# A fused attention and mixture-of-experts kernel: second expert projection with the tokens as stationary side, three weight buffers, and reordered batch boundaries

## The reference

```python
inp = _ln_c(x) + 2.0 * sinu
q, k, v = conv2d(inp, wq), conv2d(inp, wk, 1, 1), conv2d(inp, wv, 1, 1)   # 1x1, 3x3, 3x3; 8 heads of 32
q = q * cos + rotate_every_two(q) * sin                                   # k likewise
attn = softmax(einsum('bhid,bhjd->bhij', q, k) * SCALE)                   # 1024 x 1024 a head
attn = einsum('bhij,hg->bgij', attn, mix)
out = einsum('bhij,bhjd->bhid', attn, v)
a, g = split(conv2d(out, wo) + bo, 2)
x = x + a * sigmoid(g)
# experts: E = 8, hidden 512, the two best of each token
h = gelu(einsum('end,edh->enh', layernorm(t) * ln_g + ln_b, W1) + b1)     # 128 -> 512
y = einsum('enh,ehd->end', h, W2) + b2                                    # 512 -> 128
t = t + (weights * the two chosen y).sum()
```

## Time and profile before

| | us |
|---|---|
| median of three executions | 2919.08 (2915.07 to 2923.99) |
| the profiled execution, its time | 2920.96 |
| its span, first instruction to last | 2919.2 |
| PE busy | 2782.3 (95%) |
| DVE busy | 2268.1 (78%) |
| ACT busy | 1465.8 (50%) |
| POOL busy | 1385.4 (47%) |

### The profile page before, as it was taken

One profiled execution on the slowest core, in us unless ns is written; L12 is line 12 of the kernel. 1 busy time (PEld: TensorE's weight loads), 2 busy tenths in 40 slices (PEclk: granted clock), 3 DMA queues, 4 the chain that ended last, 5 costly groups with the idle time before them and its releaser, 6 DMA issues.

```text
span 2919.2 us, 51230 instructions
## 1 busy us (share of the span) xinstructions
PE 2782.3 (95%) x20202; PEld 2602.2 (89%) x20202; DVE 2268.1 (78%) x3471; ACT 1465.8 (50%) x1883; POOL 1385.4 (47%) x1049
## 2 busy tenths in 40 slices
PE   6999999999999999999999999999999999997896
PEld 5899989998999899988999899989998999976676
DVE  6777788778878888878887787888778888764563
ACT  3455445553555355544555355535554455564561
POOL 4344433544445524653354344553465336456783
PEclk9999999999999999999999999999999999998998
DMA  2555030102111120202111211112010201156665
GB/s 110 202 197 215 8 98 23 33 24 94 37 38 58 62 67 25 73 23 84 37 40 45 95 37 39 57 63 54 24 44 30 76 23 54 53 176 216 208 213 205
DMA packets 98632, 237.89 MB, mean 81 GB/s; under 512 B 19960, under 2 KB 24642, under 8 KB 98406
## 3 DMA queue, kind: packets, MB, share of 16 engines
q1 hardware_dynamic: 89318, 217.85, 23.2%
q0 software_dynamic: 9088, 16.94, 1.7%
HBM read 131.23 MB, written 105.30 MB: 81 GB/s over the span
## 4 chain that ended last, share of the span: by engine, by line
PE 74%; DVE 9%; DMA 5%; issue 4%; POOL 3%; ACT 3%; SPq 1%; another core or an unknown queue 1%; POOLq 0%; DVEq 0%; ACTq 0%
PE PV L752 48%; PE ST L752 13%; PE MX L752 12%; DMA wt<-wall 2%; POOL acc L638 1%; DVE rt L1573 1%; DMA stk<-rt 1%; DMA qst<-stk 1%; ACT xr L1215 1%; DVE El L1608 1%; DVE tmp L1587 1%; ACT h L1215 1%; PE PV L860 1%; DMA y<-yrows 1%
## 5 line engine op out<-in xcount | busy, mean ns | idle before, releaser
L638 POOL TENSOR_TENSOR acc<-acc,tmp 128x256 f32<-128x256 f32 x512 | 801.3, 1565 | 1204.3 <-DVE tmp L1618 1202.3
L752 PE MATMUL PV<-vh,El 128*128 128x258 f32 x4096 | 1186.3, 290 | 9.8 <-DVE El L1608 4.5
L752 PE MATMUL PV<-vh,Eh 128*128 128x258 f32 x4096 | 1158.0, 283 | 0.0
L752 PE MATMUL PV<-vl,Eh 128*128 128x256 f32 x4096 | 1148.8, 280 | 0.0
L1215 ACT ACTIVATE Eh<-ST 128x1024 fp32r<-128x1024 f32 x512 | 524.6, 1025 | 735.1 <-PE ST L752 735.1
L1603 DVE TENSOR_REDUCE mcol<-MX 128x1 fp32r<-128x1024 f32 x512 | 625.5, 1222 | 254.4 <-PE MX L752 253.6
L752 PEld LDWEIGHTS PV<-vh,El 128*128 128x128 f32 x4096 | 772.8, 189 | 42.7 <-issue 10.9
L752 PEld LDWEIGHTS PV<-vl,Eh 128*128 128x128 f32 x4096 | 779.9, 190 | 24.6 <-issue 3.3
L752 PEld LDWEIGHTS PV<-vh,Eh 128*128 128x128 f32 x4096 | 774.5, 189 | 0.0
L1608 DVE TENSOR_TENSOR El<-E,Eh 128x1024 fp32r<-128x1024 f32 x512 | 641.4, 1253 | 0.4
L1215 ACT ACTIVATE E<-ST 128x1024 f32<-128x1024 f32 x512 | 521.6, 1019 | 0.0
(11 more groups left out here) (264 smaller groups left out, 3357.0 us busy)
## 6 DMA issues: line engine op xcount, KB each, us to landing
rows<-xr SPq DMA_DIRECT2D x68, 520.0 KB, 6.3
stk<-rt SPq DMA_DIRECT2D x64, 512.0 KB, 2.8
kst<-stk SPq DMA_DIRECT2D x192, 128.0 KB
qst<-stk SPq DMA_DIRECT2D x192, 128.0 KB
wt<-wall SPq DMA_DIRECT2D x39, 514.0 KB
wt<-wall SPq DMA_DIRECT2D x39, 512.5 KB
xrow<-rows SPq DMA_DIRECT2D x39, 260.0 KB
y<-yrows SPq DMA_DIRECT2D x32, 256.0 KB, 4.6
```

The source lines that it names most:

```text
L638: nc.gpsimd.tensor_tensor(acc[:, ic, :], acc[:, ic, :], tmp[:, p, :], ALU.add).then_inc(s_acc, 1)
L752: return nc.tensor.matmul(o, w, m, start=start, stop=stop)
```

## The change

`project` takes the hidden layer's parts as stationary side, 128 tokens at a time, and the weights as moving side of 128 columns, so that its results are token rows in PSUM; they go to two banks in turn. `y_out` and `y_transpose` are gone. DVE's `weight_out` adds the bias, which now stands in every row of the second weights (`WROW`), and then multiplies. Both weights have three buffers, and a load waits for the last reader of its own buffer. `load_mid` goes in halves and in tiles 21 to 36. `values` takes high x high, high x low and then low x high. The order of the calls in `batch` is another on PE, ACT and DVE, and the first batch's pairs are written out. The core of the diff (left out: semaphores and buffers renamed to match, the written-out pairs on the other engines, counts):

```diff
-WROW = (2 * HID + HK, 2 * HID + 1)
+WROW = (2 * HID + HK, 2 * HID + C)
...
+WB = 3
...
-        wt = [[keep(f"wt{i}{par}", [P, WROW[i]], f32r) for par in range(2)] for i in range(2)]
+        wt = [[keep(f"wt{i}{par}", [P, WROW[i]], f32r) for par in range(WB)] for i in range(2)]
...
-        yev = [keep(f"yev{i}", [P, NB], f32) for i in range(2)]
+        ysum = [keep(f"ysum{i}", [P, NB], f32) for i in range(2)]
...
+                sp.dma_start(wall_d[1][:, :, 2 * HID:2 * HID + C],
+                             b2.rearrange("e (o d) -> e o d", o=1).to_broadcast([EXP, P, C])).then_inc(t_wst, 16)
...
+            def load_mid(i):
+                half = slice(i % 2 * NB, (i % 2 + 1) * NB)
+                sp.dma_start(mid_sb[:, i // 2, half], mid_d[i // 2, :, half]).then_inc(t_mid, 16)
...
+            for j in range(WB):
+                load_w(0, j)
+            for j in range(WB - 1):
+                load_w(1, j)
...
-                if j + 2 < NT:
+                if j + WB < NT:
                     wait(sp, t_gl, 4 * j + 4)
-                    load_w(0, j + 2)
+                    load_w(0, j + WB)
...
-                if j + 2 < NT:
-                    wait(sp, t_ye, j + 1)
-                    load_w(1, j + 2)
+                if j + WB - 1 < NT:
+                    wait(sp, t_yw, j)
+                    load_w(1, j + WB - 1)
...
-                if 8 <= j < 8 + B:
-                    load_mid(j - 8)
+                if j >= NFULL and j < NFULL + 2 * B:
+                    load_mid(j - NFULL)
...
-            def values(n, k, p, jcs):
+            def values(n, k, p, jcs, low=None):
 
                 e = k % 2
+                hi, lo = ([t[:, e, jc, p * P:(p + 1) * P] for jc in range(KC)] for t in (Eh, El))
                 for jc in jcs:
                     if jc == 0:
                         wait(pe, s_nrm, 2 * n + p + 1)
                     if p == 0 and jc % 4 == 0:
+                        wait(pe, s_ex, 2 * n + jc // 4 + 1)
+                    mm(PV[p][:, 0:VW], hi[jc], vh[:, jc, :], jc == 0, False)
+                if low is not None:
+                    pe.wait_ge(s_vlo, low)
+                for jc in jcs:
+                    mm(PV[p][:, 0:INNER], hi[jc], vl[:, jc, :], False, False)
+                for jc in jcs:
+                    if p == 0 and jc % 4 == 0:
                         wait(pe, s_lo, 2 * n + jc // 4 + 1)
-                    hi, lo = (t[:, e, jc, p * P:(p + 1) * P] for t in (Eh, El))
-                    mm(PV[p][:, 0:VW], lo, vh[:, jc, :], jc == 0, False)
-                    mm(PV[p][:, 0:INNER], hi, vl[:, jc, :], False, False)
-                    last = mm(PV[p][:, 0:VW], hi, vh[:, jc, :], False, jc == KC - 1)
+                    last = mm(PV[p][:, 0:VW], lo[jc], vh[:, jc, :], False, jc == KC - 1)
...
                 conv_q(b, 1)
+                conv_q(b, 2)
+                conv_q(b, 3)
                 if prev is not None:
                     out_transpose(prev, 0)
-                conv_q(b, 2)
-                conv_q(b, 3)
                 conv(b, 0, 0)
+                conv(b, 0, 1)
                 if prev is not None:
                     out_transpose(prev, 1)
-                conv(b, 0, 1)
-                if prev is not None:
                     out_project(prev, 0)
                 conv(b, 0, 2)
                 conv(b, 0, 3)
                 conv(b, 1, 0)
                 conv(b, 1, 1)
                 conv(b, 1, 2)
+                conv(b, 1, 3)
                 if prev is not None:
                     out_project(prev, 1)
-                conv(b, 1, 3)
                 conv(b, 2, 0)
+                conv(b, 2, 1)
+                conv(b, 2, 2)
                 if prev is not None:
                     route_in(prev)
-                conv(b, 2, 1)
-                conv(b, 2, 2)
                 conv(b, 2, 3)
                 if prev is not None:
                     pe.wait_ge(s_xr, b + 0)
...
                 conv(b, 3, 2)
+                max_scores(n + 1, 1, 0)
                 scores(n, 0, 0, b)
-                max_scores(n + 1, 1, 0)
                 conv(b, 3, 3)
+                max_scores(n + 1, 1, 1)
                 scores(n, 0, 1, b)
-                max_scores(n + 1, 1, 1)
...
-                if prev is None:
-                    with pe.Fori(0, HEADS // 2 - 1) as hp:
-                        pair(n + hp * 8, heads_next(hp), split=b * 4 + 4)
-                else:
-                    for hp in range(HEADS // 2 - 1):
-                        pair(n + hp * 8, heads_next(hp), split=b * 4 + 4, route=prev if hp == 1 else None,
-                             through=b - WPREP if hp == 2 and 0 <= b - WPREP < EXP // 2 else None)
+                for hp in range(HEADS // 2 - 1):
+                    pair(n + hp * 8, heads_next(hp), split=b * 4 + 4, route=prev if hp == 1 else None,
+                         through=b - WPREP if hp == 2 and 0 <= b - WPREP < EXP // 2 else None)
...
-            def y_transpose(j):
-                wait(pe, t_ye, j + 1)
-                wait(pe, t_yw, j)
+            def project(j):
+
+                w = wt[1][j % WB]
+                wait(pe, t_w[1][j % WB], 16 * (j // WB + 1))
+                wait(pe, t_yw, j - 1)
+                wait(pe, t_hl, 2 * j + 2)
                 for i in range(4):
-                    last = nc.tensor.transpose(YT[:, i * P:(i + 1) * P], yev[j % 2][:, i * P:(i + 1) * P], ident[:, :])
-                last.then_inc(t_yt, 1)
-
-            def project(j):
-                w = wt[1][j % 2]
-                wait(pe, t_w[1][j % 2], 16 * (j // 2 + 1))
-                wait(pe, t_ye, j)
-                for k in range(HK):
-                    if k % 2 == 0:
-                        wait(pe, t_hl, 2 * j + k // 2 + 1)
-                    last = split3(Y, w[:, k * P:(k + 1) * P], w[:, HID + k * P:HID + (k + 1) * P],
-                                  hh[:, j % 2, k, :], hl[:, j % 2, k, :], k == 0, k == HK - 1)
+                    at = slice(i * P, (i + 1) * P)
+                    for k in range(HK):
+                        last = split3(PV[j % 2][:, at], hh[:, j % 2, k, at], hl[:, j % 2, k, at],
+                                      w[:, k * P:(k + 1) * P], w[:, HID + k * P:HID + (k + 1) * P], k == 0, k == HK - 1)
                 last.then_inc(t_y, 1)
...
-                if j > 0:
-                    y_transpose(j - 1)
                 project(j)
...
                 rot_hi(b, 1)
                 if prev is not None:
                     gate_tanh(prev, 0)
+                middle_copy(b, 0)
...
                 rot_hi(b, 4)
+                rot_hi(b, 5)
                 if prev is not None:
                     gate_tanh(prev, 1)
-                rot_hi(b, 5)
...
                 rotate(b, 0)
+                rotate(b, 1)
                 if prev is not None:
                     out_lo(prev, 0)
-                rotate(b, 1)
+                rot_lo(b, 0)
+                rotate(b, 2)
                 if prev is not None:
                     clear(prev)
-                rot_lo(b, 0)
-                rotate(b, 2)
                 rot_lo(b, 1)
                 rotate(b, 3)
                 middle_sums(b, 0)
                 even_odd(b, 0, 0)
-                rot_lo(b, 2)
                 if prev is not None:
                     gate(prev, 0)
+                rot_lo(b, 2)
+                even_odd(b, 0, 1)
+                if prev is not None:
+                    out_lo(prev, 1)
                 turn(b, 4)
                 rot_lo(b, 3)
-                if prev is not None:
-                    out_lo(prev, 1)
-                even_odd(b, 0, 1)
                 turn(b, 5)
                 middle_sums(b, 1)
-                if prev is not None:
-                    gate(prev, 1)
                 rot_lo(b, 4)
                 even_odd(b, 1, 0)
                 even_odd(b, 1, 1)
                 rot_lo(b, 5)
                 turn(b, 6)
+                if prev is not None:
+                    gate(prev, 1)
                 turn(b, 7)
                 middle_sums(b, 2)
+                rot_lo(b, 6)
                 even_odd(b, 2, 0)
                 if prev is not None:
                     logits(prev)
-                rot_lo(b, 6)
                 v_lo(b, 0)
+                take_max(n, 0, 0)
+                rot_lo(b, 7)
                 even_odd(b, 2, 1)
-                take_max(n, 0, 0)
+                take_max(n, 0, 1)
                 v_lo(b, 1)
-                rot_lo(b, 7)
-                take_max(n, 0, 1)
...
             def weight_out(j):
-                wait(dve, t_yt, j + 1)
+                wait(dve, t_y, j + 1)
                 if j >= YR:
                     wait(dve, t_sc[j % YR], 64 * (j // YR))
+                y, bias = ysum[j % 2].rearrange("p (i d) -> p i d", d=C), f(wt[1][j % WB][:, 2 * HID:2 * HID + C])
+                tt(y, PV[j % 2].rearrange("p (i d) -> p i d", d=C), rows(bias, 4, C), ALU.add).then_inc(t_ys, 1)
+                wait(dve, t_ys, j + 1)
```

(54 more changed lines are left out.)

36 lines of the change are left out of this document (11 added, 25 removed).

## The result

The changed kernel takes 2937.76 us in the median of seven runs (2933.86 to 2943.49), the kernel before 2919.08 on the same chip: a ratio of 1.007, 95% interval 1.005 to 1.009. It is slower by 0.7%, where the forecast was no measurable change, at 2917 us.

What follows compares the result with a forecast made beforehand. TensorE was taken as the bound, waiting mainly at batch boundaries and for weights in the expert stage. Expert stage with tail +25.5, boundaries -27.7, the rest 0: -2.2 us, about 2917 us; range 2900 to 2942.

Steps and rivals of the forecast that it cites:

- The projection: Expert tiles: 48 narrow pairs at 0.111 us plus change-over, 5.43 us a projection, making a tile 8.7 us of PE.
- The weights: Expert stage: with a third buffer the 18.1 us of waits for weights go; the middle stretch gains some 15.
- DVE sets the start of the pairs: Rival, boundaries: PE only waits elsewhere, so they give just -10 against +32 in the expert stage; about 2941 us, chance 0.20.
- The third buffer doesn't help: Rival, middle expert tiles: transfer rate, not late issue, binds them; the middle stays near 114 us, time 2934, chance 0.08.
- the granted clock falls to 1.2 GHz in the projections: Rival, expert projections: narrow pairs take about twice 0.111 us, +5.3 us a tile, 3120 us if always; chance 0.03.
- The boundaries: Seven boundaries between batches: reordered calls and a recovered clock, less time given back, sum -27.7 us, bounds -10 and -38.
- The stack's term: Boundaries: `gate(prev, 1)` goes behind `turn(b, 6)` on DVE, so the first stack's spill is issued sooner: -10.9 us.
- the clock's 10.3 us: Boundaries: 10.3 us lost to the granted clock falling behind waits; two thirds counted as regained, -7 us.
- the low part's term: Boundaries: `values` takes the low part last and needs `vl` and `El` later, saving about half their waits: -3.7 us.
- The accumulator's: Boundaries: `conv_q` 2 and 3, six wide matmuls of 1.4 us, go under the 1.84 us accumulator wait: -9.8 us.
- The rest: First batch's loop passes written out and the bias table written once: taken as 0, between -3 and +3 us.
- The tail: Behind the last projection: POOL's scatters have caught up, so read-back comes after 7.7 us instead of 13.7: -6.0 us.

Runs made afterwards that it cites:

- e12: The changed kernel itself, run once more with nothing altered: 2936.72 us, ratio 1.0075 to the kernel before.
- e6: The changed kernel without the sixteen scatters of the last image's rows, a small memset in place of each: 2921.80 us, ratio 1.0025.
- e13: The changed kernel with the last image's sixteen scatters as plain DMAs from the same queue to a spare tensor: 2919.44 us, ratio 1.0020.
- e14: The changed kernel with fifteen more indirect scatters to a spare tensor, three a tile in tiles 24 to 28: 2952.05 us, ratio 1.0122.
- e3: The kernel before with the change's attention part and three weight buffers, loads one tile further ahead, old projection kept: 2869.19 us, ratio 0.9854.
- e5: The changed kernel with two buffers a weight in place of three: 2933.12 us, ratio 1.0064.
- e7: e3 with `values` in the order of the kernel before, low part first: 2868.75 us, ratio 0.9838.
- e9: e3 with DVE's two normalise calls ahead of the two subtractions for the next image's mixed low parts: 2862.03 us, ratio 0.9821.
- e1: The kernel before with only the attention part of the change, expert part as before: 2900.35 us, ratio 0.9947.

## Why the prediction was wrong

Against the forecast's -2.2 us the profile is 24.8 us too long: 18.3 in the expert stage, 5.5 in the pairs and 3.7 in the boundaries, less 2.8 at the start and the end. None of the prediction's three signs of being wrong came (the pitch, a wait for weights, boundaries that hardly change); only the length of the stage told. By its own steps:

**The projection** was right. The pairs follow each other at 0.111 us, 5.31 us for 48 where 5.43 was said, and a tile takes 8.56 us where 8.7 was. The late tiles, with nothing else in them, grew by 31.3 us. The Trainium skill's "TensorE: Matmul & The Clock Gate", section "Back-to-back issue gap", has about 81 ns for a pair of load and matmul at 128 columns in a sustained stream; this trace does not agree, with 0.111 us over the 48 pairs of each late tile.

**The weights** are the step that failed: "I take the waits for weights [...] as gone, and count PE's work alone", by which "the middle stretch gains some 15". The waits did go; the stretch gained nothing (113.7 to 113.6 in the profile, 106.4 in e12's). In their place PE's signals arrive late, PE stops, and the clock falls behind it, in the tiles where the last image's indirect scatters run beside those of the results. e6 and e13 show that these scatters are the cause, since without them, or with plain DMAs, the middle is 95.2 us and the whole stage within 3 us of the forecast; e14 shows that scatters added elsewhere do the same. In the ratios they cost 0.5% (1.007 to 1.0025 and 1.0020), 14 us. Without them the change comes out at 0.25% and 0.20%, within the 0.3% that the forecast called no change. That the loads were late with two buffers was right (e3); that nothing but PE's work would be left was not. The sign stood in the trace of before, not in its list of waits: ACT's `yev`, 2.4 us behind the projection that it waits for.

**The other rivals.** Two came near in time, and neither holds. "DVE sets the start of the pairs" (2941) counted -10 us for the boundaries, which gave -24.0. "The third buffer doesn't help" (2934) is false in its mechanism for the old projection: e3 moves 238 GB/s in the middle, so the rate was not the limit, and the buffer is worth 31 us to it; to the new projection it is worth nothing, since that one doesn't wait (e5). That "the granted clock falls to 1.2 GHz in the projections" is not so either: it is at 1.00 through all late tiles, and in the expert stage falls only behind holds and once in the first tiles.

**The first tiles** took 82.9 us in this profile, at a mean clock of 0.94, and 78.7 in that of e12, from the same code: the clock is the difference.

**The boundaries** were forecast at -27.7 and gave -24.0. The stack's term (-10.9) measured -9.7, `vt`'s (-3.4) -3.3; of the clock's 10.3 us all came back, where two thirds were counted. Of the low part's term (-3.7) `El`'s wait went and `vl`'s stayed at 3.8; 7.1 were given back to the row maximum, where 8.8 are waited for. The accumulator's (-9.8) was mis-sized: -2.9. Its six matmuls were put under a wait whose length isn't PE's: DVE comes to `normalise` behind two subtractions for the next image, so PE, freed sooner by the new `values`, waits that much longer (e7, e9). I had given back time ahead of the row maximum, but not here.

**The rest** was taken as 0 between -3 and +3, but the pairs cost 5.5 us, 3 or more of it by the order of `values` (e7): at a clock of 1.00 the fifth image takes 258.5 us in the table above and 257.9 in the earlier trace rows. Falls of the clock just behind a boundary don't explain it, since they lengthen the pairs of two images in either profile (259.1 and 259.4 us in before, 260.0 and 260.1 after).

**The tail** (-6.0) came out at -5.4 up to the read-back, 8.3 us where 7.7 were counted, and at -6.4 from the last projection to the end.

## What to carry to other kernels

A wait on the list names who came last, not why he was late: before a stall is costed as gone, ask of each engine in the same stretch whether its signals arrive on time (an engine idle long after the last thing it waits for has ended). Where several edits are bundled, cost each against the others' absence too: the third buffer is worth 31 us to the old projection and nothing to the new one, and by the ratios the new projection costs some 34 us with two buffers (e1 to e5) and 63 with three (e3 to the changed kernel). And a call put under a wait saves only if the wait's end is set by something that does not move with it.

## What the runs showed of the hardware

Six or seven indirect DMAs on GpSimd in a tile that takes 8.6 us undisturbed (1.27 us each, so nearly without a pause), in a stretch that moved 177 to 188 GB/s, held up what TensorE signals: ACT started 5.1 us after the transposes it waits for, and 10.3 us after the projection in e3, at 238 GB/s. TensorE itself then stopped, in the middle of a stream without a wait, and its clock fell from 2.4 to 1.2 GHz behind it. Four a tile did not do this (late stretch, 173.2 us without a wait), nor did plain DMAs of the same bytes from the same queue (e13, 95.2 us). On what path the signals are held isn't shown by these traces; and as each of these executions was recorded by the profiler, none shows whether the hold comes without the recording. The expert stage of one and the same kernel differs by 11 us from run to run: 7.2 in the middle, by the holds and the clock behind them, and 4.2 in the first tiles, by the clock.
